# A DLRM tower on one core: the gathers move from steps of four to bursts of 8, 12 and 12, and half of the second layer moves ahead of the last transposes

## The reference

```python
e = jnp.stack([tbl_0[ids[:, 0]], ..., tbl_26[ids[:, 26]]], axis=1)   # 2048 x 27 x 128
dot = jnp.einsum('bnd,bmd->bnm', e, e)
z = dot.reshape(2048, 27 * 27)[:, lower_triangle]                    # 2048 x 351
h = jnp.concatenate([z, dense_ctx], axis=1)
h = jnp.maximum(h @ W_top1 + b_top1, 0.0)                            # 512
h = jnp.maximum(h @ W_top2 + b_top2, 0.0)                            # 256
y = h @ W_top3
```

## Time and profile before

| | us |
|---|---|
| median of 3 runs | 512.14 (509.94 to 519.04) |
| profiled execution | 503.7 |
| its span, first to last instruction | 501.9 |
| TensorE busy / GpSimd busy | 377.5 / 286.9 |
| mean granted TensorE clock | 0.864 of full |

### The profile page before, as it was taken

One profiled execution on the slowest core, in us unless ns is written; L12 is line 12 of the kernel. 1 busy time (PEld: TensorE's weight loads), 2 busy tenths in 40 slices (PEclk: granted clock), 3 DMA queues, 4 the chain that ended last, 5 costly groups with the idle time before them and its releaser, 6 DMA issues.

```text
span 501.9 us, 14882 instructions
## 1 busy us (share of the span) xinstructions
PE 377.5 (75%) x6214; PEld 340.0 (68%) x6214; DVE 234.1 (47%) x505; ACT 130.5 (26%) x165; POOL 286.9 (57%) x264
## 2 busy tenths in 40 slices
PE   2578466289569977699919995699786988299997
PEld 2477356189458966499707984689675987289786
DVE  4766081257215663166612872165631636338241
ACT  2265010124012232033301340122320313123432
POOL 5888667763455744465663845467544767638300
PEclk9959579579788997799957997799967999789999
DMA  7995312212112131133122131132211231111100
GB/s 193 271 253 147 120 46 74 53 34 96 34 44 76 47 106 31 31 86 110 32 52 63 44 106 37 37 76 56 96 36 28 74 120 32 49 26 35 28 1 0
DMA packets 22270, 36.18 MB, mean 72 GB/s; under 512 B 12662, under 2 KB 13310, under 8 KB 22252
## 3 DMA queue, kind: packets, MB, share of 16 engines
q1 hardware_dynamic: 13996, 19.01, 13.2%
q0 software_dynamic: 8256, 16.92, 12.8%
HBM read 35.90 MB, written 0.01 MB: 72 GB/s over the span
## 4 chain that ended last, share of the span: by engine, by line
PE 66%; issue 21%; another core or an unknown queue 4%; DMA 3%; DVE 2%; ACT 2%; SPq 1%; ACTq 0%; DVEq 0%
PE emb_ps L693 30%; PE gram_ps L738 13%; PE mlp_ps L761 7%; PE emb_ps L729 5%; PE mlp_ps L775 3%; PE emb_ps L709 3%; DMA ids_b<-in_ids_mm 3%; PE mlp_ps L783 2%; DVE onehot L564 2%; PE emb_ps L828 1%; PE mlp_ps L745 1%; ACT embT L459 1%; SPq L276 1%; PE emb_ps L840 1%
## 5 line engine op out<-in xcount | busy, mean ns | idle before, releaser
L415 POOL DMA_INDIRECT rows<-in_tbl,idx x256 | 279.9, 1093 | 181.4 <-PE gram_ps L738 53.3
L693 PE MATMUL emb_ps<-onehot,parts 125*128 125x256 f32 x1280 | 171.8, 294 | 34.5 <-issue 15.1
L693 PEld LDWEIGHTS emb_ps<-onehot,parts 125*128 125x128 f32 x1280 | 163.7, 198 | 42.9 <-issue 22.3
L564 DVE TENSOR_SCALAR onehot<-ids_b,row_of 128x512 fp32r<-128x512 int32 x320 | 131.1, 483 | 85.7 <-PE emb_ps L693 46.8
L738 PE MATMUL gram_ps<-embT 128*32 128x26 f32 x4096 | 72.3, 217 | 79.0 <-issue 78.9
L738 PEld LDWEIGHTS gram_ps<-embT 128*32 128x32 f32 x4096 | 61.4, 136 | 93.3 <-issue 93.1
L451 ACT ACTIVATE embT<-emb_ps 128x512 f32<-128x512 f32 x40 | 49.0, 1224 | 141.4 <-PE emb_ps L693 91.6
L586 DVE STREAM_TRANSPOSE turned<-gram_ps 128x832 f32<-128x832 f32 x16 | 16.8, 1050 | 128.9 <-PE gram_ps L738 121.1
L459 ACT ACTIVATE embT<-emb_ps 128x512 f32<-128x512 f32 x32 | 36.8, 1241 | 81.2 <-PE emb_ps L729 62.8
L580 DVE COPY embT<-emb_ps 128x512 f32<-128x512 f32 x32 | 36.1, 1184 | 22.0 <-PE emb_ps L729 9.7
L729 PE MATMUL emb_ps<-ident,rows 128*128 128x128 f32 x256 | 36.2, 296 | 4.2 <-issue 3.1
(11 more groups left out here) (40 smaller groups left out, 105.7 us busy)
## 6 DMA issues: line engine op xcount, KB each, us to landing
ids_b<-in_ids_mm SPq DMA_DIRECT2D x8, 896.0 KB
ids_b<-in_ids_mm SPq DMA_DIRECT2D x16, 256.0 KB
rows<-in_tbl,idx POOLq DMA_INDIRECT x256
embT<-in_tbl SPq DMA_DIRECT2D x6, 448.0 KB
w_sb<-in_tbl SPq DMA_DIRECT2D x2, 448.0 KB
turned<-in_tbl SPq DMA_DIRECT2D x1, 560.0 KB
w_sb<-in_W_top SPq DMA_DIRECT2D x1, 512.0 KB
turned<-in_tbl SPq DMA_DIRECT2D x1, 448.0 KB
```

The lines of the kernel that those rows point to most:

```text
L415: pool.indirect_dma_start(rows[:, t, n, :], None, tables[f], bass.IndirectOffsetOnAxis(idx[:, t, f:f + 1], 0), engine_sem=gathers_written) ...
L564: last = nc.vector.tensor_scalar(onehot[:, k % OH:k % OH + LOOK_TABLES, c, :], ids_b[:, k:k + LOOK_TABLES, :], row_of[:, c:c + 1], None, A ...
L693: last = nc.tensor.matmul(emb_ps[BANK[k]][:, m * W:(m + 1) * W], parts[0:MP, f, part, c * D:(c + 1) * D], onehot[0:MP, f % OH, c, :], star ...
```

## The change

GpSimd's second waits are other ones: group 0 of tile 0 waits for Gram 0 of pass p-1, group 2 of tile 0 for Gram 1 of pass p-1, group 1 of tile 1 for the first table of lookup 3 in pass p (`s_looked`); the others have none. The wait ahead of the loop is gone. On TensorE the table of calls now counts positions ahead of a group: six calls ahead of "group 4", which is the same place as before; four calls of the second layer ahead of group 0 of tile 1 and four behind group 3.

```diff
-CALLS_AFTER = [{3: 6}, {3: 8}]
+CALLS_AT = [{NT: 6}, {0: 4, NT: 4}]
...
                 if isinstance(p, int) and p == 0:
                     return
-                if t == 0:
-                    if k == 1:
-                        pool.wait_ge(emb_filled, (p - 1) * JOBS + row_job(0, NT - 1) + 1)
-                    elif k == 2:
-                        pool.wait_ge(gram_filled, (p - 1) * TILES + 1)
-                    elif k == 3:
-                        pool.wait_ge(emb_filled, (p - 1) * JOBS + row_job(1, NT - 1) + 1)
-                elif k == 0:
-                    pool.wait_ge(gram_filled, p * TILES)
+                if t == 0 and k % 2 == 0:
+                    pool.wait_ge(gram_filled, (p - 1) * TILES + 1 + k // 2)
+                elif t and k == 1:
+                    pool.wait_ge(s_looked, looked(p, 3))
                 else:
-                    pool.wait_ge(emb_filled, p * JOBS + k)
+                    return
                 pool.sem_inc(pool_waited, 1)
...
-                if first:
-                    pool.wait_ge(gram_filled, 1)
-                    pool.sem_inc(pool_waited, 1)
...
-                    for k in range(NT):
-                        transpose_rows(p, t, k)
-                        for _ in range(0 if first else CALLS_AFTER[t].get(k, 0)):
+                    for k in range(NT + 1):
+                        for _ in range(0 if first else CALLS_AT[t].get(k, 0)):
                             (first_layer_rest, second_layer)[t](p - 1, calls)
                             calls += 1
+                        if k < NT:
+                            transpose_rows(p, t, k)
                     gram(p, t)
```

## The result

The change made the kernel 13% slower: 577.99 us (576.13 to 579.46, 4 runs) against 511.04 (506.94 to 519.04, 4 runs), ratio 1.134 [1.125, 1.142]. Forecast were 498.3 us, in a range of 486 to 530. The profiled execution took 577.14 us, its span 575.3.

A forecast was written before the change was run, and what follows sets the result against it. TensorE's program bounds the kernel, its Grams starved of instructions beside back-to-back gathers. Gains 6.9 (pass 1) + 5 x 2.6 - 6.1 (last pass) = 13.8 take 503.7 to 489.9; plus 8.4 (median over profiled), 498.3 us, range 486 to 530.

The forecast's parts named there:

- Train 1 "costed at nothing": Twelve gathers from 1.25 us into the pass to near 17.9, all beside lookups, at no cost to TensorE.
- The cover: Twelve gathers beside lookups at 158.93 to 175.33 left TensorE's records contiguous, taken as evidence that the first train costs nothing.
- rival C: First train starves lookups, at lookup 1: 9.7 us a pass lost, 44 us slower in all, 556 us; chance 0.25.
- Train 2 "caught by the tail": Twelve gathers at 20.7 to 36.6 into the pass; their tail catches Gram 0, which ends at 40.6 against 43.6.
- Rival B: TensorE's store empties before Gram 0, leaving first-layer records over: Gram 0 ends 2.8 us later; 518 us; chance 0.22.
- the forecast's 3.0 gained at Gram 0: Pass 2: Gram 0 ends 40.6 us into the pass instead of 43.6; taken as 2.6 us for the mean pass.
- Train 3 and Gram 1: Eight gathers behind Gram 0, as before; Gram 1 ends 15.2 us after Gram 0, unchanged.
- Pass 1: The opening train stops at its 20th gather, 5.0 us sooner; Gram 0 ends at 128.9 instead of 135.85, gaining 6.9.
- The last pass: Gram 0, clean before, meets gathers and ends 5.3 us later; with 0.8 for the moved layer, 6.1 lost.
- The layer's split: Moving four second-layer matmuls changes nothing except in the last pass, charged 0.8 us once, bounds 0 and 1.8.
- The reading of the gaps: TensorE gets few instructions beside back-to-back gathers; a Gram ends only after the train's end; about 15.5 us a pass lost.

The follow-up runs named there:

- e3: Changed kernel with one more wait: group 3 of tile 0 waits for lookup 0, splitting the first train into 4, a pause and 8; 523.22 us, ratio 1.035.
- e1: Kernel before with only the second layer's calls split 4 + 4, the gathers' waits as before; 511.36 us, ratio 1.010 [1.000, 1.021].
- e9: Changed kernel without the gathers, the waits for them and their index loads in passes 1 to 7; 381.49 us.
- e19: Changed kernel without GpSimd's second waits, with a memset that nothing waits for ahead of every gather; 664.12 us, ratio 1.305.
- e7: Changed kernel with two more waits: group 3 of tile 0 for lookup 0, group 2 of tile 1 for the large lookup; 500.79 us, ratio 0.987.
- e8: Changed kernel whose gathers, from pass 1 on, move 16 of 128 columns each, with as many descriptors; 574.52 us.
- e18: Changed kernel with a memset that nothing waits for ahead of every gather; 487.29 to 490.17 us and once 669.85; ratio 0.958 without that one.

## Why the prediction was wrong

**Train 1 "costed at nothing": the step that failed.** It was forecast to end near 17.9 into the pass, beside lookups, and stands there (166.3 - 149.7 = 16.6). It cost 10.0 us. The cover was the stretch of 12 gathers from 158.93 to 175.33, but that one follows a pause of 2 us and began beside one-hots, which stretch gathers to 1.57 us. Train 1 runs at 1.25 us: the one-hots that were to slow it, forecast at 7.0 into the pass, were themselves held back beside it and came at 162.23, 12.5 in. e3 shows that a pause behind the fourth gather, until lookup 0 is done, is enough, though eight gathers and then train 2 follow it. This is rival C, at its place, lookup 1, and at its price (9.7 forecast, 10.0 measured), to which I gave 0.25. I argued against it with the one-hots' start, read from a trace in which the pause stood just there. They wait for TensorE's signal of lookup 0, and with no pause that signal came late.

**Train 2 "caught by the tail": failed too.** I had it run 20.7 to 36.6 into the pass, with Gram 0 the only one to suffer. It ran 30.1 to 45.4, some nine later because the lookups were. It then met the end of the large lookup, whose signal was raised 10.3 us late; ScalarE's move waited for the signal, and the last four transposes waited 7.44 us for the move. Starvation was for me a thing of TensorE's records per microsecond; that TensorE's signals are held back too was missing, and no term of the sum stood for it. Rival B named the transposes as a place behind train 2, but by an emptied store, and priced it at 2.8 us. C's price left it out. For pass 2 it was 9.7 for train 1 and the forecast's 3.0 gained at Gram 0: +6.7. Measured were +10.0 for the lookups, +10.1 for the transposes, +2.4 for the first layer, -9.0 for a Gram 0 that meets no train, and -0.8 elsewhere: +12.7. So C gave 556 us and not 578.

**The +2.4 is the clock.** Pass 2 of the changed kernel by windows (from:to, length; busy us and count of PE, PEld, DVE, ACT, POOL; granted clock; DMA share; GB/s), the first layer and then Gram 0:

```profile
197.70:203.70 6.00, 6.00 (x16) 4.60 (x17) 4.76 (x10) 1.96 (x2) 0.00 (x0) 0.52 0.02 2
203.70:206.00 2.30, 2.30 (x258) 2.26 (x257) 0.00 (x0) 0.84 (x2) 0.00 (x0) 1.00 0.00 0
```

After 7.44 us of idle the granted clock is 0.52 of full over 6 us, so at its lower level, 1.2 GHz, for nearly all of them, and 12 records take 5.18 us where they take 2.76 at 174.17.

**Train 3 and Gram 1: right.** 15.2 us from Gram 0's end to Gram 1's, as forecast.

**Pass 1: 1.3 gained of 6.9.** Train 2 ran from 107.28 to 123.0 (forecast 109.0 to 124.9), but the transposes waited 7.40 us for ScalarE's move there too, and Gram 0 ended at 134.47, not at 128.9.

**The last pass: +13.9, forecast +6.1.** Its Gram 0 is clean; lookups 1 and 2 take 524.32 - 508.62 = 15.7 us (8.3 before: +7.4), the transposes 545.12 - 536.88 = 8.2 (3.6 before: +4.7) and the first layer behind them 4.4 (2.7 before: +1.7).

**The layer's split: right** within e1's interval.

**The reading of the gaps: right for TensorE's records, incomplete for its signals.** Gathers starve, a train's end releases (e9, e19). The rule of the Trainium skill that was weighed against it ("Runtime: NRT & Kernel Launch", section "Instruction fetch mechanics", that fetching is hidden) would have left the time at 512; the trace does not agree, whatever it is that carries the shortage. No run here shows whether it is the fetch of instructions: that wasn't tried.

## What to carry to other kernels

Ask of a train of GpSimd gathers not only which TensorE work it lies beside, but whether a pause stands ahead of that work, and for which signals of TensorE other engines wait while it runs. Twelve in a row cost 10 us here; sixteen with a pause of 2 us behind the fourth cost lookup 1 nothing (e7). Cover that you read from a trace holds only as long as what made it is itself on time; a pause that "does nothing" can be the cover. Look at the trains that come out, not at the waits that you write: gathers held back by one wait can join the next train (e3), and e7's two splits bring back the trains of the kernel before.

## What was not expected of the hardware

- Back-to-back indirect DMAs of 128 rows, 1.25 us apart, leave TensorE few records once its store is gone: in lookup 1 of pass 2 seven in 7.8 us, in Gram 0 of the kernel before 33 in 8.1 us. At 1.45 to 1.6 us apart lookups are fed; a Gram gets 5 to 6 records a microsecond in e19.
- Beside such a train the signals that TensorE's matmuls raise can come 5 to 11 us late, where they come 0.29 us behind the matmul's start without gathers (e9). The engines that wait for them look late for no reason in the view of waits.
- Bytes play no visible part: 4.08 MB in place of 16.92 leaves the time at 574.52 (one run, e8), and the signal of the large lookup as late, 10.4 us.
- Chips differ. Three gave 507 to 511 us for the kernel before, one 392.26, near e9's 381.49 without gathers. Why is open.
- One execution of e18 took 669.85 us among three at 487 to 490, at a mean granted clock of 1.00 of full; the cause is open.
